# Last FFN of a fused transformer block: two of four batches computed as 23 tiles of chosen rows, between the dense pairs of the other two

## The reference, cut to what matters

```
logits = x @ Wg                                  # 8 experts
probs = softmax(logits)
top_w, top_i = top_k(probs, 2)
top_w = top_w / (sum(top_w) + 1e-08)
combine = sum(one_hot(top_i) * top_w)            # (token, expert), 2 of 8 are not zero
h = square(relu(einsum('td,edh->teh', x, W1)))   # hidden size 256, every expert
y = einsum('teh,ehd->ted', h, W2)
out = einsum('te,ted->td', combine, y)
```

## Time and profile before

| what | value |
|---|---|
| median of 3 runs | 620.08 us |
| time of the profiled execution | 618.64 us |
| its span, first to last instruction | 616.5 us |
| PE busy | 563.0 us (91%), 4722 matmul records |
| DVE (VectorE) busy | 408.1 us (66%) |
| ACT (ScalarE) busy | 372.2 us (60%) |
| POOL busy | 216.0 us (35%) |
| mean granted PE clock | 0.986 |

### The profile page before, as it was taken

One profiled execution on the slowest core, in us unless ns is written; L12 is line 12 of the kernel. 1 busy time (PEld: TensorE's weight loads), 2 busy tenths in 40 slices (PEclk: granted clock), 3 DMA queues, 4 the chain that ended last, 5 costly groups with the idle time before them and its releaser, 6 DMA issues.

```text
span 616.5 us, 13386 instructions
## 1 busy us (share of the span) xinstructions
PE 563.0 (91%) x4722; PEld 351.7 (57%) x4722; DVE 408.1 (66%) x1436; ACT 372.2 (60%) x774; POOL 216.0 (35%) x374
## 2 busy tenths in 40 slices
PE   5899999997876899889889979999799999999997
PEld 2477767675543544445545545545455457776775
DVE  2636657589997999998677776777778144523233
ACT  5466766565420566667666567676466765666664
POOL 1302003324109966662199826876001000000000
PEclk9999999999997999999999989999899999999999
DMA  7200000000000000000000000000000000000000
GB/s 236 70 2 2 1 1 1 2 1 11 0 2 13 13 14 9 9 14 14 11 11 7 13 12 14 11 9 11 13 13 3 1 2 1 17 1 18 1 18 17
DMA packets 13169, 9.49 MB, mean 15 GB/s; under 512 B 5168, under 2 KB 12720, under 8 KB 12848
## 3 DMA queue, kind: packets, MB, share of 16 engines
q1 hardware_dynamic: 13104, 8.66, 5.0%
HBM read 4.71 MB, written 1.05 MB: 9 GB/s over the span
## 4 chain that ended last, share of the span: by engine, by line
PE 68%; DVE 21%; issue 6%; POOL 3%; ACT 2%; DVEq 0%; ACTq 0%; POOLq 0%
PE BANK L1160 16%; PE BANK L1142 16%; PE BANK L1259 5%; PE BANK L1210 4%; DVE QST L900 4%; PE BANK L1234 4%; PE BANK L1231 3%; PE BANK L1262 2%; PE BANK L1265 2%; DVE SW L854 2%; DVE M L852 2%; DVE X L836 2%; PE BANK L1274 2%; POOL OH L412 2%; PE BANK L1216 1%
## 5 line engine op out<-in xcount | busy, mean ns | idle before, releaser
L649 ACT ACTIVATE PT<-BANK 128x256 f32<-128x256 f32 (+2 forms) x352 | 158.1, 492 | 102.3 <-PE BANK L1234 80.2
L1160 PEld LDWEIGHTS BANK<-W,PT 128*128 128x128 f32 x1024 | 124.1, 192 | 30.4 <-issue 28.7
L412 POOL TENSOR_SCALAR OH<-IOTA,POS 128x128 bf16<-128x128 bf16 x240 | 139.3, 601 | 1.7 <-DVE POS L868 1.0
L1160 PE MATMUL BANK<-W,PT 128*128 128x128 f32 x1024 | 124.9, 275 | 0.0
L1142 PE MATMUL BANK<-XNT_ALL,W 128*128 128x512 f32 x256 | 120.9, 596 | 0.0
L836 DVE SCALAR_TENSOR_TENSOR X<-BANK,COMB,X 128x128 f32<-128x128 f32 x256 | 71.7, 342 | 73.1 <-PE BANK L1160 72.8
L561 ACT ACTIVATE PT<-BANK 128x512 f32<-128x512 f32 x128 | 76.1, 597 | 70.5 <-PE BANK L1142 69.9
L895 DVE CUSTOM_DVE_ANT_0 XN_a<-BANK,BANDQ 128x256 f32<-128x256 f32 (+1 forms) x128 | 62.3, 487 | 28.9 <-PE BANK L1210 27.3
L895 DVE CUSTOM_DVE_ANT_0 XN_c<-BANK,BANDQ 128x384 f32<-128x384 f32 (+1 forms) x128 | 62.2, 486 | 8.8 <-PE BANK L1210 7.8
L1142 PEld LDWEIGHTS BANK<-XNT_ALL,W 128*128 128x128 f32 x256 | 44.6, 191 | 37.4 <-issue 32.7
L1231 PE MATMUL BANK<-BANDK,IDB 128*128 128x128 bf16 x384 | 63.9, 222 | 0.6 <-ACT PT L649 0.3
(11 more groups left out here) (229 smaller groups left out, 846.5 us busy)
## 6 DMA issues: line engine op xcount, KB each, us to landing
W<-w SPq DMA_DIRECT2D x2, 1024.0 KB, 8.5
X<-x SPq DMA_DIRECT2D x4, 256.0 KB, 3.4
out<-X SPq DMA_DIRECT2D x4, 256.0 KB, 2.2
KZB<-KALL SPq DMA_DIRECT2D x20, 36.0 KB, 1.9
KZC<-KALL SPq DMA_DIRECT2D x20, 36.0 KB, 1.9
ROW<-rows SPq DMA_DIRECT2D x1, 320.0 KB, 3.1
KZB<-KALL SPq DMA_DIRECT2D x20, 8.0 KB, 1.7
KZC<-KALL SPq DMA_DIRECT2D x20, 8.0 KB, 1.7
```

Of the source, the lines that this page charges most:

```text
L412: last = nc.gpsimd.tensor_scalar(OH[g % 2][:, i, t, :], IOTA[:, :], POS[:, t, c:c + 1], None, ALU.is_equal)
L649: nc.scalar.activation(PT[u % PT_RING][:, 0:w], P2_BANK[u % SCORE_RING][:, 0:w], ACT.Exp, scale=SCALE).then_inc(S["exp_done"], 1)
L1160: last = mm(DOWN_BANK[n % 2][:, t * P:(t + 1) * P], HID_T[n % 2][hh][:, t * P:(t + 1) * P], W2[:, e, hh, :], start=(hh == 0), stop=(hh == ...
```

## The change

The last FFN computes batches 0 and 1 sparsely. Each of their 1024 rows goes to its two chosen experts alone. In DRAM a region XS of 1024 rows (plus a spare) stands for each expert; at the start it is filled with zeros by one DMA. During attention, after the gate of batch 0 (group 8) and of batch 1 (group 12), the kernel counts the rows of each expert with triangular matmuls (`route`), works out a place for each row and choice (`slots`) and a table of which 128-row tiles are used (`table`), and POOL scatters the rows of 130 values (128 of the normed x, the weight, the row's number) with 16 indirect DMAs, 128 rows each, in groups 10, 11, 13 and 14. With two choices per row and up to 127 unused places per expert there are at most 23 tiles, and always 23 are computed.

In the last FFN, SP loads each tile's rows and its expert's W1 and W2 (copied from SBUF to a ring of eight tiles, at an index read from the table). PE transposes the tile, up and down follow, DVE scales by the weight, and POOL writes the rows to a second DRAM tensor YT at their own numbers. After the last tile SP loads YT back as two addends for each of batches 0 and 1, and DVE adds them to X (`add_experts`) after pairs 14 and 15. The dense pairs are those of batches 2 and 3, 16 in all; pairs 0 to 10 have two tiles each beside them and pair 11 has one. Dense downs use one bank instead of two, since the tiles need banks of their own (T_BANK, U_BANK x 2, D_BANK).

The gate in groups 8 and 12 is split into six parts, at units 4 to 9. W1, W2 and one tile of zeros lie in one SBUF tensor, W12. Some constants share the room of other tensors.

The diff, cut to its core (words in parentheses stand for code that is described there):

```diff
+WAVE = 2
+JT = WAVE * T
+NT = (2 * JT * P + E * (P - 1)) // P
+REGION = JT * P
+SLOTS = E * REGION + P
+ROW_W = D + 2
+IN_RING, Y_RING = 8, 4
+DENSE = (B - WAVE) * E
+TWO_TILES = 11
+GATE_AT, GATE_PARTS = 4, 6
+ROUTE_AT, TABLE_AT = 11, (15, 18, 20)
+SUM_AT = {14: 0, 15: 1}
...
+def routed(g):
+    return g // GROUPS - 2 if g % GROUPS == 0 and g // GROUPS - 2 in range(WAVE) else None
+def tile_steps(m):
+    first = 2 * min(m, TWO_TILES) + max(m - TWO_TILES, 0)
+    count = 2 if m < TWO_TILES else 1
+    return [i for i in range(first, first + count) if i < NT]
...
@@ SyncE @@
+            sp.wait_ge(S["act_zero1"], 1)
+            per, reps = SLOTS * ROW_W // P, 25
+            sp.dma_start(XS..., W12[:, E, 0:per // reps] broadcast reps times).then_inc(S["zeroed"], 16)
...
-            for b in range(B):
-                sp.wait_ge(F[1]["acc"], b * E + E)
+            sp.wait_ge(S["r_table"], 1)
+            sp.wait_ge(S["scattered"], 16 * 2 * JT)
...
+            sp.wait_ge(S["p2_done"], (NG - 2) * UNITS)
+            for n in range(NT):
+                slot = n % IN_RING
+                row = sp.value_load(TABLE[0:1, n:n + 1], min_val=0, max_val=E * JT)
+                if n == HG:
+                    sp.wait_ge(S["p2_done"], (NG - 1) * UNITS)
+                if n >= IN_RING:
+                    sp.wait_ge(S["tile_y"], n - IN_RING + 1)
+                sp.dma_start(XT_IN[slot], XS[tile at row]).then_inc(TILE_IN[slot], 16)
+                sp.dma_start(WST[slot][:, :], W12[:, expert row // JT, :]).then_inc(TILE_IN[slot], 16)
+            sp.wait_ge(F[1]["acc"], E)
+            store(WAVE)
+            sp.wait_ge(S["p2_done"], NG * UNITS)
+            for slot in range(Y_RING):
+                sp.wait_ge(Y_OUT[slot], 16 * slot_count(slot))
+            for b in range(WAVE):
+                for k in range(2):
+                    sp.dma_start(YB[b][k], YT[...]).then_inc(Y_IN[b], 16)
+            for b in range(WAVE):
+                sp.wait_ge(S["x_sum"], b + 1)
+                store(b)
+            sp.wait_ge(F[1]["acc"], DENSE)
+            store(B - 1)
@@ GpSimd @@
+            def scatter(b, n):
+                j, k = b * T + n // 2, n % 2
...
+                nc.gpsimd.indirect_dma_start(XS[:, :], IndirectOffsetOnAxis(IDX[:, k, j:j + 1]), XROW[:, k, j, :], ...)
+            def tile_out(n):
+                slot = n % Y_RING
+                pool.wait_ge(S["tile_y"], n + 1)
+                nc.gpsimd.indirect_dma_start(YT[:, :], IndirectOffsetOnAxis(IDY[:, slot:slot + 1]), YST[slot], ...)
...
+                for a in range(WAVE):
+                    lo = T * (g - GROUPS * a - 2 * GROUPS - 2 + a)
+                    if 0 <= lo < 2 * T:
+                        for n in range(lo, lo + T):
+                            scatter(a, n)
             attended(NG - 1)
-            rstd("t", B - 1)
+            for n in range(NT):
+                tile_out(n)
+                if n == 5:
+                    rstd("t", B - 1)
@@ ScalarE @@
+                    if b < WAVE:
+                        nc.scalar.copy(XROW[:, 1, j, 0:D], XROW[:, 0, j, 0:D]).then_inc(S["g_twice"], 1)
...
+            zero(W12[:, E, :])
             for st in (*QST, *KST):
...
+            def tile_copy(n):
+                act.wait_ge(S["tile_t"], n + 1)
+                nc.scalar.copy(XTS[n % 2], T_BANK[:, 0:P]).then_inc(S["tile_xt"], 1)
+            def tile_hidden(n):
+                act.wait_ge(S["tile_up"], n + 1)
+                nc.scalar.activation(TR[n % 2], U_BANK[n % 2][:, 0:HID], ACT.Relu).then_inc(S["tile_relu"], 1)
+                if n >= 2:
+                    act.wait_ge(S["tile_down"], n - 1)
+                act.wait_ge(S["tile_relu"], n + 1)
+                nc.scalar.activation(TH[n % 2], TR[n % 2], ACT.Square).then_inc(S["tile_sq"], 1)
+            def tile_step(i):
+                if i + 1 < NT:
+                    tile_copy(i + 1)
+                tile_hidden(i)
...
+            tile_copy(0)
+            hidden(0)
+            for m in range(DENSE):
+                steps = tile_steps(m)
+                for i in steps[0:1]:
+                    tile_step(i)
+                if m + 1 < DENSE:
+                    hidden(m + 1)
+                if m in (1, 4):
+                    tail(B - 1, 0 if m == 1 else 2)
+                for i in steps[1:]:
+                    tile_step(i)
+                if m == 5:
                     t_exp(B - 1)
@@ VectorE @@
...
-                    if u == 4 and g % GROUPS == 0 and b >= 1:
-                        tail(b - 1, 4)
+                    if GATE_AT <= u < GATE_AT + GATE_PARTS and g % GROUPS == 0 and b >= 1:
+                        gate_part("t", b - 1, u - GATE_AT)
+                    if routed(g) is not None and u == ROUTE_AT + 1:
+                        slots(routed(g))
+                    if routed(g) == WAVE - 1 and u in TABLE_AT:
+                        table(TABLE_AT.index(u))
...
+            def tile_y(n):
+                slot, row = n % Y_RING, XT_IN[n % IN_RING]
+                dve.wait_ge(S["tile_down"], n + 1)
+                if n >= Y_RING:
+                    dve.wait_ge(Y_OUT[slot], 16 * (n // Y_RING))
+                nc.vector.tensor_scalar(IDY[:, slot:slot + 1], row[:, D + 1:D + 2], float(UNUSED), None, ALU.add)
+                nc.vector.tensor_scalar(YST[slot], D_BANK[:, 0:D], row[:, D:D + 1], None, ALU.mult).then_inc(S["tile_y"], 1)
...
+            for m in range(DENSE):
+                b, e = WAVE + m // E, m % E
+                steps = tile_steps(m)
+                for i in steps[0:1]:
+                    tile_y(i)
...
+                dve.wait_ge(s["down"], m + 1)
+                (4 scalar_tensor_tensor from DOWN_BANK[0], as line 836)
+                for i in steps[1:]:
+                    tile_y(i)
+                (tail(B - 1, k), as before)
+                if m in SUM_AT:
+                    add_experts(SUM_AT[m])
@@ TensorE @@
+            def route(b):
+                j0 = b * T
+                pe.wait_ge(S["r_mask"], b + 1)
+                pe.wait_ge(S["misc_free"], free("route", b))
+                for t in range(T):
+                    for j in range(j0 + t, -1, -1):
+                        last = mm(MISC[:, t * E:(t + 1) * E], TRI[:, 0 if j == j0 + t else 1, :], MSK[:, j, :], ...)
+                if b == WAVE - 1:
+                    for j in range(JT):
+                        last = mm(MISC[:, T * E:T * E + E], TRI[:, 1, :], MSK[:, j, :], ...)
+            def tile_turn(n):
+                pe.wait_ge(TILE_IN[n % IN_RING], 32 * (n // IN_RING + 1))
+                if n:
+                    pe.wait_ge(S["tile_xt"], n)
+                nc.tensor.transpose(T_BANK[:, 0:P], XT_IN[n % IN_RING][:, 0:D], IDENT[:, :]).then_inc(S["tile_t"], 1)
+            def tile_up(n):
+                pe.wait_ge(S["tile_xt"], n + 1)
+                if n >= 2:
+                    pe.wait_ge(S["tile_relu"], n - 1)
+                (2 matmuls of 128 columns: W1 half of WST x XTS -> U_BANK[n % 2])
+            def tile_down(n):
+                pe.wait_ge(S["tile_sq"], n + 1)
+                if n:
+                    pe.wait_ge(S["tile_y"], n)
+                (2 matmuls of 128 columns: TH x W2 half of WST -> D_BANK)
+            def tile_step(i):
+                if i + 1 < NT:
+                    tile_up(i + 1)
+                if i + 2 < NT:
+                    tile_turn(i + 2)
+                tile_down(i)
...
             pv(NG - 1, T + 1)
+            tile_turn(0)
+            tile_up(0)
             norm(NG - 1)
...
+            up(0)
+            tile_turn(1)
+            for m in range(DENSE):
...
+                if m + 1 < DENSE:
+                    up(m + 1)
+                for i in steps[0:1]:
+                    tile_step(i)
+                pe.wait_ge(s["square"], m + 1)
+                pe.wait_ge(s["square_act"], m + 1)
+                pe.wait_ge(s["acc"], m)
+                (16 records into DOWN_BANK[0], as line 1160)
+                k = {1: 0, 2: 1, 4: 2, 5: 3}.get(m)
+                if k is not None:
+                    tail(B - 1, k)
+                for i in steps[1:]:
+                    tile_step(i)
```

More of the change, by code:

```diff
@@ L223, in build @@
         KALL = [sb(f"KALL{n}", [P, KW], F16) for n in range(2)]
+        KZ_LATER = [[sb(f"KZ{n}{i}", [P, L]) for i in range(HG)] for n in "BC"]
         KZ = [[r[:, :].bitcast(F16) for r in (QS, VS, PR, HXT)],
-              [sb(f"KZB{i}", [P, L])[:, :].bitcast(F16) for i in range(HG)],
-              [sb(f"KZC{i}", [P, L])[:, :].bitcast(F16) for i in range(HG)]]
+              *([r[:, :].bitcast(F16) for r in later] for later in KZ_LATER)]
         VSEL = [sb(f"VSEL{n}", [P, HG, SLOT]) for n in range(3)]
@@ L261, in build @@
              for f in range(2)]
+        TILE_IN = [S[f"tile_in{n}"] for n in range(IN_RING)]
+        Y_OUT = [S[f"y_out{n}"] for n in range(Y_RING)]
+        Y_IN = [S["y_in0"], S["y_in1"]]
         KEYS_IN = [S["keys_in0"], S["keys_in1"]]
@@ L1112, in tail @@
```

(3 more changed lines are left out.)

277 lines of the change are left out of this document (226 added, 51 removed).

## The result

The changed kernel takes 602.48 us in the median of 4 runs (601.84 to 604.32), the kernel before 620.06; the ratio is 0.972, 95% interval 0.9698 to 0.9743. That is 17.6 us faster, inside the forecast's range, and 9.5 us above its number (593). The profiled execution took 602.45 us with a span of 600.4, 16.1 less than the 616.5 of before.

What follows compares the result with a forecast made beforehand. PE's records were taken to bound the last FFN, DVE's gate bursts groups 8 and 12. Terms -56.1, +23.0, +1.1, +2.5, +3.2, -1.3, +0.35 make -27.25: 591.4 against the profiled 618.64, 592.8 for the median, said as 593; range 587 to 603.

Steps and rivals of the forecast that it cites:

- Parts 1 to 4: Last FFN: 16 dense pairs go -56.1, 23 tiles +23.0, side DMAs hidden 0, start +1.1, tail copies +2.5, end +3.2.
- Rival A: Last FFN, the forecast itself: PE sets the woven pairs; own range 588 to 598, chance 0.66.
- rival B: Woven pairs: a tile's chain shows, ACT, DVE or a landing late by 0.5 to 1.3 us; +10, 603; chance 0.21.
- D: Last FFN: POOL's indirect DMAs pace the tiles, slower from 4.5 us each; at 5, +12, 632; chance 0.05.
- E: Woven pairs: clock at 0.50 for a third to half of their time, 615 to 626; chance 0.03.
- Part 5: Attention: gate in six parts, routing added; group 8 -2.4, group 12 +0.9, two ACT copies +0.2; sum -1.3.
- Part 3: DMAs beside the tiles, and scatters in groups 10, 11, 13, 14 behind POOL's sums of heads: hidden, cost 0.
- Part 6: First 30 us: ACT's zeroing copy ahead of the warming matmuls delays the first real one, +0.35; the rest 0.

Runs made afterwards that it cites:

- before_split: The kernel before, with only its gate cut into five parts in units 4 to 8 of groups 8 and 12: 614.37 us (0.993).
- best2: Changed kernel with route in unit 5 of groups 9 and 13, table in group 14, copies and gate parts moved, three last-FFN edits: 589.50 us (0.9527).
- the first four experiments: Run on one chip: changed kernel with route three units later (598.17 us), routing in groups 9 and 13 (598.05), gate in one burst (603.26); before_split (614.37).
- again: The changed kernel, not edited, profiled a second time on a second chip: 604.01 us (0.9739).
- gate_burst: The changed kernel with the gate of batches 0 and 1 in one burst in unit 4 again: 603.26 us (0.9748).
- route_next: The changed kernel with route, slots and table in groups 9 and 13 instead of 8 and 12: 598.05 us (0.9663); 602.24 us on a third chip.

## Why the prediction was right or wrong

**Right, the last FFN (Parts 1 to 4).** Forecast -26.3, measured -26.1. PE sets the pairs, at the 5.5 us said (5.51 in pairs 3 and 7 to 9, where no tail work stands); from the first up to the last addition it is 88.9 us for the 88 said; a tile is 1.00 us; ACT's tail copy shows in pairs 1 and 4; the last downs wait 1.31 for the forecast 1.35; the two additions take 1.37 for 1.4. Sizes off: the tail's copy costs 0.84 a pair as a wait, not 1.25; at the start the first up is 0.78 later, 0.55 of it the first tile's five records, so 0.23 where 0.5 was forecast, and pair 0 takes 6.12 us without a wait that shows.

**Inside the range by luck.** Rival A was the case, and its own range of 588 to 598 was too low at the top: its bound for attention was +2, and groups 8 and 12 alone brought +5.2. The time lies inside 587 to 603 because the range had room for rival B, which did not happen.

**Right, no gap rule.** The Trainium skill's page TensorE: Matmul & The Clock Gate, "Back-to-back issue gap", would by the prediction's estimate from its figures have made the tiles some 28 us dearer. The traces disagree with it for these f32 products, as the rows of before did: nine records of 128 columns in 1.00 us.

**Rivals B, D, E.** A tile's chain shows only in the three waits above, 2.4 us in all (B). An indirect DMA of a tile occupies POOL for 0.97 us, and with the 0.30 of issue seen between the scatters that is 1.27 for the 1.3 taken; POOL waits 40 us of the stage for DVE's rows (D). The clock is 1.00 until PE's last product; the 0.98 of the stage comes from a fall at 596.8, behind it (E).

**Wrong, Part 5.** The failing step is "with the gate in six parts the waits are short", and with it -2.4 for group 8 and +0.9 for group 12. The demands were not too small: DVE 18.46 and 20.43 us busy for 18.8 and 22.4, PE 18.84 and 20.36 for 18.4 and 20.0, a part of it at half clock. But a group's length was taken as the larger demand, and the order of the one bank was not followed. The route was costed by its matmuls (0.6 and 2.2 us) and not as a user of MISC, placed two units behind a user that DVE frees. before_split shows the forecast's own half (-2.7, -2.5), best2 what the routing costs at a place with room: 0.2 us in groups 8 and 12, 0.4 in 9, 0.4 in 14, and 1.5 in 13, stall included. In place of -1.5 the two groups brought +5.2: 6.7 of the 11.05 us between the sum's 591.4 and the profiled 602.45. The stalls below are 3.4 of it, the first stretch 0.8.

**Wrong, the scatters at nothing.** The cover that Part 3 names is there (no wait for POOL's sums of heads shows), and yet groups 10, 11, 13 and 15 lost 3.6 us where Part 5 had 0.2 for two copies. On the chip of the first four experiments they lost nothing, so this term was right there. The stalls stand behind rows of four scatters, that of group 15 behind those of group 14.

**Part 6, +0.35.** ACT's zeroing copy does delay the warming matmuls, to 6.48 from 5.95, but the first real one starts at 9.78 instead of 9.76: the term was nothing. What comes behind it can't be read. After reached group 1 at 222.75, before at 221.68, and again, the same kernel as after, at 225.24; gate_burst at 221.47.

**What would have avoided it:** list for each new instruction the buffer that it takes, who frees the buffer, and how far that engine runs behind.

## What to carry to other kernels

A new step in a software pipeline has to be placed by the distances between users of its buffer, not by idle time of its engine: here the counting two units behind a use that DVE frees, with the work that hangs on it, cost 2 us without any backlog (group 9), and 2 to 5 with the gate beside it (after against route_next); in unit 5, with four units to the next user and ACT's copies pulled ahead of it, it cost 0.4 (group 9 of best2). Work that is spread to avoid a burst must also be laid beside what the neighbour engine does: DVE's small SBUF operations against POOL's large ones. Issue GpSimd's scatters two at a time where a row of four brings a stall; one kernel on one chip shows the gain.
